# Two score tiles ahead of the first maxima unit in a fused attention and expert kernel

## The chip, the cores and the metric

The kernel runs on one core of one Trainium2 chip. The metric is the device time of one execution in microseconds (us), the median of several. Three executions of the kernel before took 356.44, 356.56 and 356.78 us.

## What is computed

Two layers for a batch of 2. First a cross attention with residual: the 512 tokens of `x` of each batch, normalised, are the queries; keys and values come from the 154 normalised context rows and the same normalised tokens (666 in all), with 16 heads of 64. Then a mixture of 8 experts with residual, where each token goes to its two best experts. The change touches the attention alone, which per batch is

```
q = lat @ Wq;  k, v = split(concat([ctx, lat]) @ Wkv)      # 16 heads of 64
attn = softmax(q @ k.T * 64**-0.5);  x = x + (attn @ v) @ Wout
```

## The kernel before, in words

**Steps.** The attention is worked off in `STEPS` = 16 steps, each a pair of heads of one batch (8 pairs, 2 batches). The scores of a step are kept transposed: keys on the partitions, 512 queries along the free axis. The 666 keys are cut into `KT` = 6 tiles of 111 (`KP`). Each engine runs its own instruction list, written by hand, in order; the lists meet only by semaphores. A step on TensorE has two phases.

**First phase** (L468 to L473). For each key tile `kt`, `dots(s, kt)` (L348) makes the scores of both heads in one of two PSUM buffers, `sc[:, kt % 2]`: six matmuls of 512 columns (L362, two heads of 64 rows each, three products of high and low parts), then two matmuls (L368) that add the negated row maxima of step s. ScalarE then takes the exponent of that tile (`exponent`, L636). Because there are two buffers, `dots(s, kt)` waits at its head until the exponent of tile `kt - 2` is done (L355). After each tile stands one unit of `lead_next(s + 1, u)` (L330, matmuls L326): a rough product of queries and keys of the *next* step, from which VectorE reduces the next step's row maxima (`reduce_max`, L767 and L771). A unit writes `mx` when `u` is even and `xo` when odd. Units 0 to 3 cover 444 keys for 128 queries (two matmuls, one per head); units 4 and 5 cover the other 222 keys for twice 128 queries (four matmuls). From unit 2 on, a unit waits until the reduction of unit `u - 2`, which reads the same buffer, is done (L340: `max_done` at `n * UNITS + u - 1`).

**Second phase.** For steps 0 to 13: `project_q` and `project_k` of step s + 2 (L295 to L297, into the score buffers), then part of a values projection (`project_v`, into `mx`, after the reduction of unit 4, L491). Step 14 has `out_project` (L460, into `mx`) there instead, after the same reduction (L486). Then `turn_max` (L345), which transposes the maxima once VectorE has joined them (`join_max`, L777); `total` (L389); and the six `pv` tiles (L382), the product of exponents and values.

**The other engines in a step.** VectorE: six reductions, `join_max`, low parts of q and k (L751, L758), `spread_max` (L782), four reciprocals (L796). ScalarE: a copy of the previous output (L640), six exponents, copies of q, k and v (L617, L621, L626), a copy of the sums (L646). GpSimd adds up the exponents (`gather`, L1050), normalises (L1057) and splits weights. Step 15 has score tiles but no maxima units between them. After it come the experts.

Of the kernel before, what the change touches and what calls it, by code (L numbers as in the profile page):

```python
# [29 lines left out]
KT = 6  # L30
# [21 lines left out]
def pair_of(s):  # L52
    return 2 * (s // 4) + s % 2
# [6 lines left out]
def v_half(s):  # L60

    n = s // 2 + 1
    return (n, s % 2) if n < STEPS // 2 else None


def v_count(n, half):
    return n * 2 + half + 1


def xattn_moe(nc, x, ctx_in, g_m, b_m, g_l, b_l, wq, wkv, wout, wg, w1, b1, w2, b2, out):  # L70
    with ExitStack() as stack:
# [221 lines left out]
        def _(pe):  # L293
# [5 lines left out]
            def project_q(n, bank=sc[:, 0, 0, :]):  # L299
                b, w = batch_of(n), pair_of(n) % 2  # L300
                three(bank, wqk_hi[:, w, 0, :], wqk_lo[:, w, 0, :], kv_hi[:, b, 0:N], kv_lo[:, b, 0:N]) \
                    .then_inc(q_ready, 1)

            def project_k(n, half, bank):
                b, w = batch_of(n), pair_of(n) % 2
                three(bank[:, 0:k_width(half)], wqk_hi[:, w, 1, :], wqk_lo[:, w, 1, :], kv_hi[:, b, k_cols(half)],
                      kv_lo[:, b, k_cols(half)]).then_inc(k_ready, 1)

            def project_v(n, half, banks=mx):
                b, w = n % B, n // B % 2  # L310
                to = banks.rearrange("p h n -> p (h n)")
                for i in range(VH):
                    kt = half * VH + i
                    at = slice(kt * KP, (kt + 1) * KP)
                    mm = three(to[0:KP, i * 2 * P:(i + 1) * 2 * P], kv_hi[:, b, at], kv_lo[:, b, at],
                               wv_hi[:, w, :], wv_lo[:, w, :])
                mm.then_inc(v_ready, 1)

            def lead(n, u, banks):
                pe.wait_ge(k_hi_done, 2 * n + (1 if u < QT else 2))  # L320
                tiles = [u] if u < QT else [2 * (u - QT), 2 * (u - QT) + 1]
                for i, t in enumerate(tiles):
                    for h in range(2):
                        r = slice(h * HD, (h + 1) * HD)
                        to = banks[:, h, 0:KW] if u < QT else banks[:, h, i * KR:(i + 1) * KR]
                        mm = pe.matmul(to, q_pair[r, n % QKB, 0, t * P:(t + 1) * P],  # L326
                                       k_pair[r, n % QKB, 0, k_cols(u >= QT)], start=True, stop=True)
                mm.then_inc(mx_ready, 1)

            def lead_next(n, u):  # L330
                if u == 0:
                    pe.wait_ge(q_hi_done, n + 1)
                    if n >= 2 and v_half(n - 2):
                        pe.wait_ge(v_copied, v_count(*v_half(n - 2)))
                elif u == 1 and n >= 2:
                    pe.wait_ge(o_copied, n - 1)
                    if n >= 3:
                        pe.wait_ge(sum_copied, n - 2)
                elif u >= 2:
                    pe.wait_ge(max_done, n * UNITS + u - 1)  # L340
                lead(n, u, xo if u % 2 else mx)

            def turn_max(n, bank=sc[:, 1, 1, :]):
                pe.wait_ge(neg_ready, n + 1)
                pe.transpose(bank[:, 0:P], neg_max[:, :, :].rearrange("p h c -> p (h c)"), ident[:, :]) \  # L345
                  .then_inc(neg_turned, 1)

            def dots(s, kt):  # L348
                if kt == 0:
                    later = min(s + 2, STEPS) if s >= 1 else 1  # L350
                    pe.wait_ge(q_lo_done, later)
                    pe.wait_ge(k_lo_done, 2 * later)
                e = s * KT + kt
                if e >= 2:
                    pe.wait_ge(exp_done, e - 1)  # L355
                if kt == 1 and s >= 1:
                    pe.wait_ge(row_done, s + 1)
                at = slice(kt * KP, (kt + 1) * KP)
                for k_part, q_part in ((0, 0), (0, 1), (1, 0)):
                    for h in range(2):  # L360
                        r = slice(h * HD, (h + 1) * HD)
                        pe.matmul(sc[0:KP, kt % 2, h, :], k_pair[r, s % QKB, k_part, at],  # L362
                                  q_pair[r, s % QKB, q_part, :], start=(k_part + q_part == 0), stop=False)
                if kt == 0:
                    pe.wait_ge(row_done, s + 1)
                for h in range(2):
                    r = slice(h * HD, (h + 1) * HD)
                    mm = pe.matmul(sc[0:KP, kt % 2, h, :], ones_r[r, :], max_row[r, s % 2, :],  # L368
                                   start=False, stop=True)
                mm.then_inc(shifted, 1)  # L370
# [15 lines left out]
            def total(s, bank=pj):  # L386
                pe.wait_ge(added, (KT - 1) * (s + 1))
                for h in range(2):
                    mm = pe.matmul(bank[h * HD:(h + 1) * HD, :], ones[0:KP, :], psum_acc[0:KP, s % 2, h, :],  # L389
                                   start=True, stop=True)  # L390
                mm.then_inc(sum_ready, 1)
# [62 lines left out]
            def out_project(b, bank, pairs):  # L454
                pe.wait_ge(o_norm, STEPS - 6)
                for t in range(QT):
                    for r in pairs:
                        if t == 0 and r >= PAIRS - 2:
                            pe.wait_ge(o_norm, (STEPS if b else STEPS - 2) - (PAIRS - 1 - r))
                        mm = pe.matmul(bank[:, t * P:(t + 1) * P], o_t[:, b, r, t * P:(t + 1) * P],  # L460
                                       wout_sb[:, r, :], start=(t == 0 and r == 0),
                                       stop=(t == QT - 1 and r == PAIRS - 1))
                if r == PAIRS - 1:
                    mm.then_inc(out_proj, 1)

            for s in range(STEPS - 1):
                made = s + 2 < STEPS
                for kt in range(KT):  # L468
                    dots(s, kt)
                    if s == 0 and kt == 0:  # L470
                        pe.wait_ge(q_lo_done, 2)
                        pe.wait_ge(k_lo_done, 4)
                    lead_next(s + 1, kt)  # L473
                if made:
                    pe.wait_ge(exp_done, s * KT + KT - 1)
                    if s % 4 in (2, 3):
                        pe.wait_ge(wqk_split, pair_of(s + 2))
                    if s == 0:
                        pe.wait_ge(kv_lo_ready, 2 * B)
                    project_q(s + 2)  # L480
                    project_k(s + 2, 0, sc[:, 0, 1, :])
                    pe.wait_ge(exp_done, s * KT + KT)
                    project_k(s + 2, 1, sc[:, 1, 0, :])
                else:
                    pe.wait_ge(tail_loaded, 16 * 4)
                    pe.wait_ge(max_done, (s + 2) * UNITS - 1)  # L486
                    out_project(0, x1_ps[0], range(PAIRS - 2))
                if v_half(s):
                    if s % 4 == 2:
                        pe.wait_ge(wv_split, s // 4 + 1)  # L490
                    pe.wait_ge(max_done, (s + 2) * UNITS - 1)  # L491
                    if s == 0:
                        project_v(0, 1)
                    else:
                        project_v(*v_half(s))
                pe.wait_ge(exp_done, s * KT + KT)
                turn_max(s + 1)
                if s >= 1:
                    total(s - 1)
                for kt in range(KT):  # L500
                    if s == 0 and kt == VH:
                        pe.wait_ge(v_copied, v_count(0, 1))
                        project_v(1, 0)
                    pv(s, kt)
# [66 lines left out]
            s = STEPS - 1  # L571
# [539 lines left out]
```

## Time and profile before

| what | us |
|---|---|
| median of three executions | 356.56 |
| the profiled execution, device time | 356.89 |
| its span, first to last instruction | 355.1 |
| TensorE matmul busy in the span | 342.6 (96%) |
| VectorE, GpSimd, ScalarE busy | 240.2, 240.7, 181.2 |
| steps 2 to 14, from pv to pv | 16.24 each, step 14 18.9 |

The profile lists for each instruction group when it ran, for how long, and in brackets how long its engine was idle before it and what ended that. PE is TensorE's matmuls, PEld its weight loads, DVE VectorE, ACT ScalarE, POOL GpSimd. Neighbouring matmuls overlap: a matmul of 512 columns is shown as some 0.39 us long while the next of its kind starts 0.23 us after it. So the profile can call TensorE busy throughout and still hold gaps between starts.

### The profile page before, as it was taken

The numbers are of one execution on the slowest core, as the hardware profiler recorded it, in microseconds if no ns is written. First come the engines' busy times: TensorE is split into PE (matmuls) and PEld (weight loads), VectorE is DVE, ScalarE is ACT, GpSimd is POOL, SyncE is SP. The second block draws the span as 40 slices with busy tenths as digits, with TensorE's granted clock in tenths as the row PEclk, the third lists the DMA queues.
The fourth block names the chain that finished last, engine by engine and source line by source line (L and its number), as shares of the span: only waits on it lengthen the run. The fifth ranks groups of instructions, "written<-read, shape, count | busy, mean of one in ns | idle before, by whom it ended". The sixth has DMA issues, their size and how long they took to land.

```text
span 355.1 us, 6060 instructions
## 1 busy us (share of the span) xinstructions
PE 342.6 (96%) x2343; PEld 231.0 (65%) x2343; DVE 240.2 (68%) x418; ACT 181.2 (51%) x240; POOL 240.7 (68%) x160
## 2 busy tenths in 40 slices
PE   2879999999999999999999999999999999999996
PEld 2758574656657474756556474747584559999986
DVE  4789286878677686868686776968744488257433
ACT  2247383755648383836556383838433553135341
POOL 3577586979797989999798989779695661010000
PEclk9999999999999999999999999999999999999999
DMA  3044000000001010010100000000000000000000
GB/s 122 0 145 124 2 14 2 2 2 0 2 0 31 0 31 15 2 30 2 30 3 16 0 2 2 0 2 0 2 0 2 1 0 3 2 0 2 30 2 30
DMA packets 6713, 5.81 MB, mean 16 GB/s; under 512 B 743, under 2 KB 5789, under 8 KB 6685
## 3 DMA queue, kind: packets, MB, share of 16 engines
q1 hardware_dynamic: 6389, 5.29, 5.0%
q8 instruction: 19, 0.31, 0.3%
q10 hardware_dynamic: 296, 0.13, 0.1%
q14 instruction: 9, 0.07, 0.1%
HBM read 4.89 MB, written 0.52 MB: 15 GB/s over the span
## 4 chain that ended last, share of the span: by engine, by line
PE 94%; DVE 3%; DMA 1%; ACT 1%; ACTq 1%; issue 0%; DVEq 0%
PE xo L382 23%; PE sc L362 20%; PE mx L564 8%; PE sc L368 6%; PE sc L295 5%; PE xo L389 5%; PE sc L297 4%; PE sc L296 4%; PE mx L326 3%; PE xo L326 3%; PE mx L460 2%; PE xo L460 2%; PE mx L295 2%; PE mx L297 2%; PE mx L296 2%; DVE part_max L767 1%
## 5 line engine op out<-in xcount | busy, mean ns | idle before, releaser
L1050 POOL TENSOR_TENSOR psum_acc<-psum_acc,probs 111x1024 f32<-111x1024 f32 x63 | 150.0, 2380 | 7.2 <-DVE psum_acc L790 2.5
L636 ACT ACTIVATE probs<-sc 111x1024 f32<-111x1024 f32 x96 | 98.3, 1027 | 21.3 <-PE sc L368 13.9
L362 PE MATMUL sc<-q_pair,k_pair 64*111 64x512 f32 x576 | 85.7, 401 | 1.0 <-ACT v_sb L626 0.8
L382 PE MATMUL xo<-probs,v_sb 111*64 111x512 f32 x384 | 85.6, 593 | 0.0
L362 PEld LDWEIGHTS sc<-q_pair,k_pair 64*111 64x111 f32 x576 | 44.6, 170 | 28.4 <-issue 12.2
L767 DVE TENSOR_REDUCE part_max<-mx 128x2 f32<-128x888 f32 x32 | 34.7, 1084 | 41.0 <-PE mx L326 39.6
L382 PEld LDWEIGHTS xo<-probs,v_sb 111*64 111x64 f32 x384 | 27.3, 137 | 53.6 <-issue 53.2
L796 DVE RECIPROCAL recips<-recips 128x128 f32<-128x128 f32 x64 | 54.3, 910 | 9.4 <-ACT recips L646 9.4
L1050 POOL TENSOR_TENSOR psum_acc<-probs 111x1024 f32<-111x1024 f32 x16 | 38.4, 2398 | 30.7 <-ACT probs L636 30.7
L640 ACT COPY o_t<-xo 128x512 f32<-128x512 f32 x16 | 9.4, 588 | 66.6 <-PE xo L382 66.6
L368 PE MATMUL sc<-max_row,ones_r 64*111 64x512 f32 x192 | 38.1, 390 | 0.0
L703 ACT ACTIVATE probs<-sc,cols 128x512 f32<-128x512 f32 x32 | 21.5, 687 | 28.3 <-PE sc L297 28.0
L767 DVE TENSOR_REDUCE part_max<-xo 128x2 f32<-128x888 f32 x30 | 32.5, 1084 | 1.4
L941 DVE SCALAR_TENSOR_TENSOR x_tok<-mx,score,x_tok 128x128 f32<-128x128 f32 x62 | 17.5, 344 | 22.1 <-PE mx L564 21.9
L564 PEld LDWEIGHTS mx<-w_sb,probs 128*128 128x128 f32 x248 | 29.9, 192 | 2.0 <-issue 0.8
L564 PE MATMUL mx<-w_sb,probs 128*128 128x128 f32 x248 | 30.2, 275 | 0.0
L1057 POOL TENSOR_TENSOR o_t<-o_t,recips 128x512 f32<-128x512 f32 x16 | 20.5, 1278 | 11.2 <-DVE recips L796 11.2
L368 PEld LDWEIGHTS sc<-max_row,ones_r 64*111 64x111 f32 x192 | 16.9, 170 | 5.5
L326 PE MATMUL mx<-k_pair,q_pair 64*128 64x444 f32 (+1 forms) x128 | 18.3, 320 | 1.3 <-DVE part_max L767 0.5
L771 DVE TENSOR_REDUCE part_max<-mx 128x4 f32<-128x888 f32 x16 | 17.3, 1082 | 1.4
L626 ACT COPY v_sb<-mx 111x768 f32<-111x768 f32 x15 | 12.0, 799 | 12.0 <-PE mx L297 12.0
L389 PE MATMUL xo<-psum_acc,ones 111*64 111x512 f32 x64 | 17.3, 618 | 0.0
(169 smaller groups left out, 478.9 us busy)
## 6 DMA issues: line engine op xcount, KB each, us to landing
w_raw<-in_L_ffn_W SPq DMA_DIRECT2D x8, 128.0 KB, 2.0
x_tok<-in_x SPq DMA_DIRECT2D x2, 256.0 KB, 3.4
wv_raw<-in_L_xattn_Wkv SPq DMA_DIRECT2D x4, 128.0 KB, 2.8
wout_sb<-in_L_xattn_Wout SPq DMA_DIRECT2D x1, 512.0 KB
wqk_raw<-in_L_xattn_Wq SPq DMA_DIRECT2D x7, 64.0 KB, 2.0
wqk_raw<-in_L_xattn_Wkv SPq DMA_DIRECT2D x7, 64.0 KB, 2.0
out<-x_tok SPq DMA_DIRECT2D x1, 256.0 KB, 2.0
out<-x_tok SPq DMA_DIRECT2D x2, 128.0 KB, 1.7
```

The lines of the kernel that those rows point to most:

```text
L295: pe.matmul(out_ap, st_hi, mv_hi, start=True, stop=False)
L326: mm = pe.matmul(to, q_pair[r, n % QKB, 0, t * P:(t + 1) * P], k_pair[r, n % QKB, 0, k_cols(u >= QT)], start=True, stop=True)
L362: pe.matmul(sc[0:KP, kt % 2, h, :], k_pair[r, s % QKB, k_part, at], q_pair[r, s % QKB, q_part, :], start=(k_part + q_part == 0), stop=False)
L368: mm = pe.matmul(sc[0:KP, kt % 2, h, :], ones_r[r, :], max_row[r, s % 2, :], start=False, stop=True)
L382: mm = pe.matmul(o_ps[h * HD:(h + 1) * HD, :], v_sb[0:KP, s // 2 % 2, kt, at:at + HD], probs[0:KP, e % RING, h, :], start=(kt == 0), stop= ...
L389: mm = pe.matmul(bank[h * HD:(h + 1) * HD, :], ones[0:KP, :], psum_acc[0:KP, s % 2, h, :], start=True, stop=True)
L564: mm = pe.matmul(y_ps(g, t)[:, t * P:(t + 1) * P], relu_ring[:, (g * HC + c) % FR, t * P:(t + 1) * P], w2_sb[:, e * HC + c, :], start=(c = ...
L636: act.activation(probs[0:KP, e % RING, :, :], sc[0:KP, kt % 2, :, :], ACT.Exp).then_inc(exp_done, 1)
L703: act.activation(relu_ring[:, n % FR, :], hid_ps[:, n % 4, :], ACT.Relu, bias=cols[:, n % (E * HC):n % (E * HC) + 1]).then_inc(relu_done, 1)
L767: dve.tensor_reduce(part_max[:, 0, :, u], banks[:, :, 0:KW], AX.X, ALU.max, negate=True) \
L796: dve.reciprocal(at, at).then_inc(recip_done, 1)
L1050: pool.tensor_tensor(psum_acc[0:KP, s % 2, :, :], first, probs[0:KP, e % RING, :, :], ALU.add) \
```

## The change

In steps 1 to 14 the first phase starts with two score tiles, and each maxima unit stands one place later; the last two units, 4 and 5, follow tile 5 one after the other. Step 0 keeps its order. No instruction is added or removed, and no other engine's list is changed.

```diff
             for s in range(STEPS - 1):
                 made = s + 2 < STEPS
-                for kt in range(KT):
+                ahead = 2 if s else 1
+                for kt in range(ahead - 1):
+                    dots(s, kt)
+                for kt in range(ahead - 1, KT):
                     dots(s, kt)
                     if s == 0 and kt == 0:
                         pe.wait_ge(q_lo_done, 2)
                         pe.wait_ge(k_lo_done, 4)
-                    lead_next(s + 1, kt)
+                    lead_next(s + 1, kt - ahead + 1)
+                if ahead == 2:
+                    lead_next(s + 1, KT - 1)
                 if made:
```

## Rows read from the trace of the kernel before

**Rows 1.** Page: busy time of each engine; chain of work that ended last, by engine
```profile
PE 342.6 (96%) x2343; PEld 231.0 (65%) x2343; DVE 240.2 (68%) x418; ACT 181.2 (51%) x240; POOL 240.7 (68%) x160
...
PE 94%; DVE 3%; DMA 1%; ACT 1%; ACTq 1%; issue 0%; DVEq 0%
```

**Rows 2.** Windows of one step each: length, then busy us of each engine, clock
```profile
74.31:90.56 16.25, 16.25 (x114) 9.81 (x113) 12.27 (x15) 9.51 (x12) 14.21 (x9) 1.00 0.00 1
...
106.80:123.03 16.23, 16.23 (x114) 9.88 (x113) 12.27 (x15) 9.52 (x12) 14.18 (x10) 1.00 0.06 17
```

**Rows 3.** Timeline of one middle step, first phase, TensorE: start us, length us, engine, line
```profile
107.53 0.40 PE L368 MATMUL sc<-max_row,ones_r 64*111 64x512 f32 x2
...
108.89 0.39 PE L326 MATMUL xo<-k_pair,q_pair 64*128 64x444 f32 x2
109.05 0.51 PEld L362 LDWEIGHTS sc<-q_pair,k_pair 64*111 64x111 f32 x6 [0.18 <-ACT probs L636]
109.09 0.91 PE L362 MATMUL sc<-q_pair,k_pair 64*111 64x512 f32 x6
...
112.58 0.85 PE L362 MATMUL sc<-q_pair,k_pair 64*111 64x512 f32 x6
...
113.50 0.38 PE L326 MATMUL xo<-k_pair,q_pair 64*128 64x222 f32 x4
...
113.81 0.50 PE L295 MATMUL sc<-kv_hi,wqk_hi 128*128 128x512 f32 x1
```

**Rows 4.** Chain of waits over the same phase: start of each piece, its length
```profile
107.93 0.20 PE mx L326 x2
108.13 0.70 PE sc L362 x6
108.84 0.23 PE sc L368 x2
109.07 0.20 PE xo L326 x2
109.27 0.73 PE sc L362 x6
...
112.53 0.22 PE mx L326 x4
```

**Rows 5.** Timeline, same step, ScalarE and VectorE in and behind the first phase
```profile
107.97 1.03 ACT L636 ACTIVATE probs<-sc 111x1024 f32<-111x1024 f32 x1 [0.53 <-PE sc L368]
...
112.79 1.08 DVE L771 TENSOR_REDUCE part_max<-mx 128x4 f32<-128x888 f32 x1
...
115.04 0.17 DVE L777 TENSOR_REDUCE neg_max<-part_max 128x8 f32<-128x16 f32 x1
...
116.61 0.27 PE L345 MATMUL sc<-ident,neg_max 128*128 128x128 f32 x1
```

**Rows 6.** Timeline of step 15, two score tiles with no maxima unit between
```profile
272.70 0.39 PE L368 MATMUL sc<-max_row,ones_r 64*111 64x512 f32 x2
...
273.14 1.03 ACT L636 ACTIVATE probs<-sc 111x1024 f32<-111x1024 f32 x1 [0.52 <-PE sc L368]
...
273.63 0.38 PE L368 MATMUL sc<-max_row,ones_r 64*111 64x512 f32 x2
274.21 0.50 PEld L362 LDWEIGHTS sc<-q_pair,k_pair 64*111 64x111 f32 x6 [0.64 <-ACT probs L636]
274.21 0.94 PE L362 MATMUL sc<-q_pair,k_pair 64*111 64x512 f32 x6 [0.20 <-ACT probs L636]
...
275.00 0.40 PE L368 MATMUL sc<-max_row,ones_r 64*111 64x512 f32 x2
```

**Rows 7.** Timeline at the start: a maxima unit held by the reduction before it
```profile
18.66 1.07 DVE L767 TENSOR_REDUCE part_max<-mx 128x2 f32<-128x888 f32 x1
...
19.79 0.48 PE L326 MATMUL mx<-k_pair,q_pair 64*128 64x222 f32 x4 [0.52 <-DVE part_max L767]
20.20 0.44 PE L407 MATMUL sc<-ident,normed 128*128 128x128 f32 x2
```

**Rows 8.** Timeline of step 14, end of its first phase
```profile
258.94 1.08 DVE L771 TENSOR_REDUCE part_max<-mx 128x4 f32<-128x888 f32 x1
...
260.12 0.46 PE L460 MATMUL mx<-wout_sb,o_t 128*128 128x128 f32 x2
```

## The prediction

> **What bounds the kernel now.** I read the page's busy times and its chain first, then windows of single steps, then the timeline of one first phase. TensorE is busy for 342.6 us and carries 94% of the chain that ended last [rows 1]. In the step windows the reader is to see that the matmul row fills all 16.24 us, while the fullest other engine, GpSimd, fills 14.2, VectorE 12.3 and ScalarE 9.5, and that the granted clock is 1.00, the 2.4 GHz level [rows 2]. So a step is as long as TensorE's stream, and a reordering can only win what TensorE loses between starts. The timeline shows where it loses a little: in front of a score tile the weight load was held for the exponent of the tile two before (0.18 us on the load's row), and the matmul behind it began only 0.04 us after the load (109.05 and 109.09) [rows 3]. In the chain the tile so held took 0.73 us for its six matmuls where an unheld one took 0.70 [rows 4]. Four tiles per step can be held in this way, so that there is at most about 0.13 us per step to win.
>
> **What the change moves.** Nothing is added: the same matmuls and weight loads, no DMA, no queue other than TensorE's. Tile 1 goes ahead of unit 0; units 0 to 4 each come one place later; units 4 and 5 meet at the end. The wait that tile 1 carries for the spread maxima is met by then, as tile 0's last matmuls wait for the same semaphore. That edit costs nothing. I follow the times of the middle step of rows 3.
>
> *Hold one, tile 2 behind exponent 0.* Tile 0's last matmuls end at 107.53 + 0.40 = 107.93 [rows 3]; exponent 0 runs from 107.97 for 1.03, to 109.00 [rows 5]. Neither moves. Tile 1 now follows at once. Step 15 already has this order, and there tile 1's last matmuls start 273.63 - 272.70 = 0.93 after tile 0's [rows 6]. So here they start at 108.46. Unit 0 starts 0.23 later (the chain's step of a score pair [rows 4]), at 108.69, and tile 2 could start 0.20 after that (the chain's step of a unit), at 108.89. But it must wait for exponent 0. Before, the load that was so released started at 109.05 [rows 3], 0.05 after the exponent's end; in step 15 it was 274.21 against 273.14 + 1.03 = 274.17 [rows 6]. So tile 2 starts at 109.05, the very time of before. A tile that starts from a hold needs, by step 15, 275.00 + 0.40 - 274.21 = 1.19 to its end [rows 6], so tile 2 ends at 110.24; before, its pieces ended at 109.27 + 0.73 + 0.23 = 110.23 [rows 4]. The time saved by having one unit less ahead of tile 2 is thus lost whole, and the unit has still to be paid: every later tile keeps its time, and the phase ends with one unit more. Cost: the 0.20 that a unit takes in the chain, per step. Bounds: nothing at all if tile 2 could start without the hold, 0.30 if the restart from a longer stop is worse than in step 15. I take 0.20.
>
> *Tiles 3 to 5.* After tile 2 the stream is again tile, unit, tile, with units 1, 2, 3 in the places where 2, 3, 4 stood. Exponent 1 may start up to 0.2 earlier, which removes a hold of some hundredths at tile 3; exponent 2 and tile 4 hang on tile 2's end and do not move. I count the gain at nothing; what hides it is the chain tile 2, exponent 2, tile 4, and at most 0.05 per step would come out.
>
> *Hold two, unit 5 behind the reduction of unit 3.* Unit 3 now sits behind tile 4, where unit 4's four short matmuls were, which in the chain started at 112.53 [rows 4]. Unit 3 ends there at 112.53 + 0.20 = 112.73. Its reduction starts 0.04 later (unit 4's did: 112.53 + 0.22 = 112.75 against 112.79) and takes 1.08 [rows 5]: to 113.85. Unit 4 starts at 113.50 in the place of unit 5 [rows 3], and its own reduction to wait for, of unit 2, ended over a unit's pitch before, near 112.7: free. Unit 5 could start 0.21 later, at 113.71, but needs the reduction of unit 3. The nearest row for such a release is the start of the kernel, where a reduction ended at 18.66 + 1.07 = 19.73 and the held unit started at 19.79 [rows 7]. So unit 5 starts at about 113.90: a hold of 0.19. And its restart is slow: there the next instruction started 20.20 - 19.79 = 0.41 after the held unit [rows 7], where a flowing one gives 113.81 - 113.50 = 0.31 [rows 3]. So `project_q` starts at 113.90 + 0.41 = 114.31 and not at 113.81: 0.50 later in all, 0.20 from hold one and 0.30 from hold two. For hold two the bounds are 0 (if the reduction were already done) and 0.40; I take 0.30. Queued behind unit 5 on TensorE is everything of the second phase, and ScalarE's and VectorE's copies of q and k wait for that.
>
> *A rule on restarts.* In the row of step 15 the matmul of a held tile and its weight load carry the same start, 274.21, and the load engine had been idle for 0.64 [rows 6]: the weights were not loaded during the hold. The Trainium skill, page "TensorE: Matmul & The Clock Gate", section "Step-by-step: what each phase is for", says that TensorE's queue pulls weight loads ahead of matmuls in flight. Were that so behind a hold as well, both restarts would lose the 0.10 of slow start, and the sum would fall to 13 x 0.30 + 1.1 = 5.0. The row speaks against it, as the wait sits ahead of the load.
>
> *Second phase.* The reductions of units 4 and 5 come late: unit 4 ends at about 113.88, its reduction runs to 114.99, unit 5's to 116.1, and the join of 0.17 ends near 116.3 instead of 115.21 [rows 5]. The transpose of the maxima stood at 116.61 [rows 5] and stands at 117.11 now, so that 0.8 are left. The values projection before it needs the reduction of unit 4 (114.99) and starts after 115.9. Both waits stay hidden. The reciprocals and the spreading end over 3 us before VectorE is wanted again. GpSimd, with 14.2 of 16.2, gets more room. Nothing in the second phase can give the 0.50 back, as TensorE's row has no wait there.
>
> *Step 14* has the output projection behind unit 5, which waits for the reduction of unit 4. Before, that ran from 258.94 to 260.02 and the matmuls started at 260.12 [rows 8], already held. Now unit 4 takes unit 5's place, whose start in the chain's terms is 1.13 later; its reduction ends at 261.15 and the projection starts at 261.25. Cost 1.13, which contains both holds. Bounds 0.20 and 1.3.
>
> **Sum.** Steps 1 to 13: 13 x 0.50 = 6.5. Step 14: 1.1. Together 7.6 us. On the profiled execution, 356.89 (its span 355.1 and 1.8 around it), that is 364.5; it was 0.33 above the median, so against the median 364.2.
>
> **The rivals.**
>
> *A: both holds, as above,* 364.2; its own range is 362.5 to 365.5 (0.1 per step either way on 14 steps). Chance 0.76.
>
> *B: only hold one.* If the reductions ran a little ahead of what I reconstruct, unit 5 would find its buffer free. For: VectorE is busy for only 12.3 of 16.2 [rows 2]. Against: the reduction of unit 3 cannot start before unit 3 is computed, and 1.08 behind that is later than 113.71. Time: 13 x 0.20 + 1.1 = 3.7, so 360.3. Chance 0.08.
>
> *C: restarts cost nothing,* as the rule above would have it: 5.0, so 361.6. Chance 0.05.
>
> *D: faster.* In ends rather than starts hold one hardly exists: exponent 0 ends 0.04 + 1.03 after tile 0, and tile 1 with unit 0 takes 0.93 + 0.20, so that tile 2 would just find it done. If the hold were then no more than the ones of before, each later tile would run unheld and the 0.13 per step of small holds would come out: 14 x 0.13 = 1.8, so 354.8. It decides from the point at which exponent 0 is visible before 108.89. Against it speaks step 15, where the held start follows the exponent's end by 0.04 although the matmuls before were still draining. Chance 0.05.
>
> *E: worse.* The join of the maxima, 1.1 later on VectorE, becomes what TensorE waits for at the transpose. It decides once the join ends after 117.1, that is if the 0.8 of slack is lost, for instance because VectorE starts on q's low part first; its list excludes that order, but a further slip of each reduction would do. Price another 0.5 per step, so 371. Chance 0.06.
>
> **Chances and range.** A difference of 0.2% (0.7 us) is about what a measurement of this kernel can tell from none. Faster by more: 0.05, all of D. Within it: 0.02, between D and B. Slower: 0.93. The range of 360.2 to 366.2 holds A, B and C and leaves out D and E.
>
> **What would show it.** Right: a step of 16.74 in place of 16.24; in each middle first phase one idle of TensorE of about 0.2 ahead of tile 2, ended by the exponent (L636), and one of about 0.2 ahead of unit 5 (L326 on `xo`), ended by the reduction (L767); the first phase's length 7.57 in place of 7.07; step 14's projection (L460) starting 1.1 later relative to its step. Wrong: tile 2 starting before 109.0 relative to this step (D), unit 5 with no idle ahead of it (B), a new wait at L345 (E), the unheld pitch right behind a hold (C). A step that isn't longer than 16.24 would overturn the whole argument.

## The result and the profile after

| | before | changed |
|---|---|---|
| median of 6 executions, us | 356.67 | 364.49 |
| lowest, highest | 356.44, 356.82 | 364.37, 366.59 |
| step pitch, steps 1 to 13 | 16.24 | 16.75 |
| step 14, sums of step 13 to sums of step 14 | 19.02 | 20.19 |

The ratio is 1.0229, with a 95% interval of 1.0217 to 1.024: slower by 7.8 us, where 7.6 had been forecast (364.2). The pitch is read from the chain of waits, where each step's `total` is one piece. The first and the last of the thirteen pieces that bound twelve steps are, after the change, with step 14's behind them,

```profile
54.37 1.01 PE xo L389 x4
...
255.33 1.01 PE xo L389 x4
...
275.52 1.01 PE xo L389 x4
```

so (255.33 - 54.37) / 12 = 16.75; before, the same pieces start at 51.94 and 246.81. The twelve steps are 2 to 13; step 1, from its first tile to its sums, takes 10.60 against 10.10 before, so it loses the same. 13 x (16.75 - 16.24) + (20.19 - 19.02) = 7.8, the whole of the measured difference. That the two agree to a tenth is in part luck: step 1's first tile starts at 41.77 in the profile before and at 41.25 in that of a later run, `not_in_step_14`, whose step 0 is the same, so the start of the kernel alone differs by half a microsecond from one profiled execution to another. Behind step 14 the two kernels take the same time: from step 15's first tile to the end 83.2 us before, 83.1 after.

The page after, busy times and chain, answers to [rows 1]:

```profile
PE 351.5 (96%) x2343; PEld 233.1 (64%) x2343; DVE 237.7 (65%) x418; ACT 179.9 (49%) x240; POOL 240.7 (66%) x160
...
PE 93%; DVE 3%; DMA 1%; ACT 1%; issue 1%; ACTq 1%; DVEq 0%
```

One step's window after, answering to [rows 2]: 16.71 of 16.75 us are called busy. The extra half microsecond shows as almost no idle, because a held matmul's predecessor is drawn as still running.

```profile
77.25:94.00 16.75, 16.71 (x113) 9.87 (x113) 12.08 (x15) 9.41 (x12) 14.13 (x9) 1.00 0.00 1
```

The timeline of the same middle step, 3.92 us later on this trace's clock than in [rows 3] (start, length, engine, line, in brackets the idle before and what ended it):

```profile
111.88 1.95 ACT L641 ACTIVATE probs<-sc 111x1024 f32<-111x1024 f32 x2 [0.52 <-PE sc L368]
112.37 0.39 PE L368 MATMUL sc<-max_row,ones_r 64*111 64x512 f32 x2
112.60 0.36 PE L326 MATMUL mx<-k_pair,q_pair 64*128 64x444 f32 x2
112.96 0.94 PE L362 MATMUL sc<-q_pair,k_pair 64*111 64x512 f32 x6
...
112.96 0.50 PEld L362 LDWEIGHTS sc<-q_pair,k_pair 64*111 64x111 f32 x6 [0.40 <-ACT probs L641]
...
116.69 1.08 DVE L772 TENSOR_REDUCE part_max<-xo 128x2 f32<-128x888 f32 x1
...
117.42 0.38 PE L326 MATMUL mx<-k_pair,q_pair 64*128 64x222 f32 x4
117.83 0.30 PEld L326 LDWEIGHTS xo<-k_pair,q_pair 64*128 64x128 f32 x4 [0.22 <-DVE part_max L772]
117.83 0.48 PE L326 MATMUL xo<-k_pair,q_pair 64*128 64x222 f32 x4
...
118.24 0.50 PE L295 MATMUL sc<-kv_hi,wqk_hi 128*128 128x512 f32 x1
```

Both holds stand where the forecast put them. Unit 0 starts at 112.60 and tile 2 not 0.20 but 0.36 later, at 112.96; less 3.92 that is 109.04, within 0.01 of the time at which its load was released before (109.05). Unit 5 starts 0.41 after unit 4 and not 0.21; the reduction of unit 3 ended at 117.77. The projection follows unit 5 by 0.41: 118.24, less 3.92 114.32, where the forecast had 114.31 and the kernel before 113.81.

The chain tells it by pieces; against [rows 4], where a held tile took 0.73:

```profile
112.76 0.20 PE mx L326 x2
112.97 0.94 PE sc L362 x6
...
117.58 0.21 PE mx L326 x4
117.79 0.04 issue
117.83 0.48 PE xo L326 x4
```

### The profile page after: what moved, and what is told of

It reads as the page before. It is cut to its first block, busy times and chain, and to the rows that moved or that the text cites. A ratio compares the mean times of both kernels' runs of the same rounds, so it can differ in the third digit from the quotient of the medians.

```text
span 364.8 us, 6060 instructions
## 1 busy us (share of the span) xinstructions
PE 351.5 (96%) x2343; PEld 233.1 (64%) x2343; DVE 237.7 (65%) x418; ACT 179.9 (49%) x240; POOL 240.7 (66%) x160
## 4 chain that ended last, share of the span: by engine, by line
PE 93%; DVE 3%; DMA 1%; ACT 1%; issue 1%; ACTq 1%; DVEq 0%
PE xo L382 23%; PE sc L362 20%; PE mx L569 7%; PE sc L368 6%; PE sc L295 5%; PE xo L389 4%; PE sc L297 4%; PE sc L296 4%; PE xo L326 4%; PE mx L326 3%; PE mx L460 2%; PE xo L460 2%; PE mx L295 2%; PE mx L297 2%; PE mx L296 1%; DVE part_max L772 1%
## 5 line engine op out<-in xcount | busy, mean ns | idle before, releaser
L641 ACT ACTIVATE probs<-sc 111x1024 f32<-111x1024 f32 x96 | 96.9, 1027 | 23.6 <-PE sc L368 18.6
L362 PE MATMUL sc<-q_pair,k_pair 64*111 64x512 f32 x576 | 87.3, 408 | 0.9 <-ACT v_sb L631 0.7
L362 PEld LDWEIGHTS sc<-q_pair,k_pair 64*111 64x111 f32 x576 | 45.9, 173 | 33.4 <-issue 12.2
L326 PE MATMUL xo<-k_pair,q_pair 64*128 64x444 f32 (+1 forms) x120 | 18.0, 338 | 0.5
```

What stands on the lines that cost most here:

```text
L641: act.activation(probs[0:KP, e % RING, :, :], sc[0:KP, kt % 2, :, :], ACT.Exp).then_inc(exp_done, 1)
```

## The experiments

My theory: the loss of a step is the sum of two holds, hold one of tile 2 behind exponent 0 (0.20) and hold two of unit 5 behind the reduction of unit 3 (0.30 with its restart), and step 14 pays for the late reduction of unit 4. Rivals were a price of the order itself (two tiles or two units side by side), and holds that overlap. Each time below stands beside the kernel before, which was 356.8 beside them.

**The pair of units moved to after tile 2.** In place of the change's loop, for this and the next experiment with k = 2 and k = 1:

```diff
-                ahead = 2 if s else 1
-                for kt in range(ahead - 1):
-                    dots(s, kt)
-                for kt in range(ahead - 1, KT):
+                unit = 0
+                for kt in range(KT):
                     dots(s, kt)
...
-                    lead_next(s + 1, kt - ahead + 1)
-                if ahead == 2:
-                    lead_next(s + 1, KT - 1)
+                    for _ in range(1 if s == 0 else {0: 0, k: 2}.get(kt, 1)):
+                        lead_next(s + 1, unit)
+                        unit += 1
```

> The order of the change, but units 1 and 2 both follow tile 2, so that only unit 0 and unit 1 stand one place later and the last units stand as before. Theory of two holds: hold one (tile 2 behind exponent 0) stays with 0.20 us per step, hold two (unit 5 behind the reduction of unit 3) is gone, unit 2 just finds its reduction done. 14 x 0.20 = 2.8 over 356.7, so 359.4; step pitch 16.44. Rival, the cost comes from a phase that ends with two units: then this is as fast as before, 356.7. Rival, every displaced unit waits a little for its reduction: a third of the loss, 359.3 as well, but with idles ended by VectorE and none by ScalarE.

Measured 363.67, ratio 1.018 (1.0146 to 1.0214), pitch 16.72. The expectation missed by 4.3 us. The timeline of the pair's neighbourhood shows why:

```profile
112.10 0.36 PE L326 MATMUL xo<-k_pair,q_pair 64*128 64x444 f32 x2
112.27 0.19 PEld L326 LDWEIGHTS mx<-k_pair,q_pair 64*128 64x128 f32 x2 [0.21 <-DVE part_max L770]
112.30 0.45 PE L326 MATMUL mx<-k_pair,q_pair 64*128 64x444 f32 x2
...
112.51 1.08 DVE L770 TENSOR_REDUCE part_max<-xo 128x2 f32<-128x888 f32 x1 [0.29 <-PE xo L326]
112.58 0.85 PE L362 MATMUL sc<-q_pair,k_pair 64*111 64x512 f32 x6
...
113.28 0.40 PE L368 MATMUL sc<-max_row,ones_r 64*111 64x512 f32 x2
...
113.65 0.47 PE L326 MATMUL xo<-k_pair,q_pair 64*128 64x444 f32 x2
```

Unit 1 is made at 112.10, its reduction ends at 113.59, and unit 3, which writes the same buffer and would have come 0.23 after the matmuls of 113.28, at 113.51, starts at 113.65 and restarts slowly: the tile behind it comes 0.31 later (113.96) in place of 0.20. Unit 2, on time at 112.30, had its load held for the reduction of unit 0, and the tile behind it comes 0.28 later. I had followed units 2 and 0 and not unit 3 and unit 1. So the hold by a reduction isn't special to the end of the phase: a unit needs some 1.5 us from its start to that of the one two places on (0.36 for itself, 1.08 for the reduction, and the two handovers), and where two units meet with no tile between, one tile is missing from that room.

**The pair after tile 1.**

> Units 0 and 1 both follow tile 1, and from tile 2 on all is as before; the two score tiles still stand together. Theory: tile 2 has its old distance from tile 0, so no idle ended by the exponent ahead of it, and the unheld pitch; but unit 0 is computed 0.9 later, its reduction ends near 110.17 on the scale of the middle step, and unit 2, two places behind, is held by 0.2 and restarts 0.1 slowly; some 0.1 comes back from exponent holds that vanish. 14 x 0.2 = 2.8, so 359.5, with the idle ended by VectorE (L772). Rival, the exponent is all that matters in a first phase: 356.7 or up to 0.05 less per step, 356.0.

Measured 360.36, ratio 1.0089 (1.0056 to 1.0123), pitch 16.51, with 0.27 lost per step where I had said 0.2. The trace shows unit 2 held, by VectorE:

```profile
125.78 0.37 PE L326 MATMUL mx<-k_pair,q_pair 64*128 64x444 f32 x2
...
126.19 1.08 DVE L770 TENSOR_REDUCE part_max<-mx 128x2 f32<-128x888 f32 x1 [3.38 <-PE mx L326]
...
126.98 0.39 PE L368 MATMUL sc<-max_row,ones_r 64*111 64x512 f32 x2
...
127.32 0.19 PEld L326 LDWEIGHTS mx<-k_pair,q_pair 64*128 64x128 f32 x2 [0.43 <-DVE part_max L770]
127.33 0.47 PE L326 MATMUL mx<-k_pair,q_pair 64*128 64x444 f32 x2
```

Unit 2 comes 0.35 after tile 2's last matmuls in place of 0.23, and the tile behind it 0.30 later in place of 0.20: 0.22 of the 0.27. Tile 2 itself takes 0.80 in the chain, and the 0.1 that I had expected back didn't come. Tile 2 no longer pays hold one, but the reduction holds unit 2: this kernel has hold two's kind alone, and the rival that only the exponent matters falls.

**Hold two taken out of the changed kernel.** `n` is the step whose maxima are reduced, one ahead of the step that TensorE is in, so the short reduction acts from step 1 on.

```diff
-                    dve.tensor_reduce(part_max[:, 0, :, u], banks[:, :, 0:KW], AX.X, ALU.max, negate=True) \
+                    dve.tensor_reduce(part_max[:, 0, :, u], banks[:, :, 0:KW // 2 if u == 3 and n >= 2 else KW], AX.X, ALU.max, negate=True) \
```

> The changed kernel, but the reduction of unit 3 reads only half of its 444 columns in steps 2 and later; it leaves out the maxima over the other half. Theory: that reduction takes about 0.6 us in place of 1.08, unit 5 finds its buffer free, 0.30 per step come out of steps 1 to 13 and step 14 keeps its loss: 364.5 - 13 x 0.30 = 360.6, step pitch 16.45. Rival, the end of the phase is slow because two units of four short matmuls stand together: 364.5 stays.

Measured 360.75, ratio 1.0109 (1.0067 to 1.0151), pitch 16.46. The shortened reduction takes 0.62, and unit 5 now follows unit 4 by 0.21 with no idle, as the timeline has it:

```profile
113.36 0.62 DVE L772 TENSOR_REDUCE part_max<-xo 128x2 f32<-128x444 f32 x1
...
114.10 0.38 PE L326 MATMUL mx<-k_pair,q_pair 64*128 64x222 f32 x4
...
114.31 0.39 PE L326 MATMUL xo<-k_pair,q_pair 64*128 64x222 f32 x4
...
114.63 0.50 PE L295 MATMUL sc<-kv_hi,wqk_hi 128*128 128x512 f32 x1
```

Hold two is thus worth 0.28 per step (16.747 - 16.463), and two units side by side cost nothing in themselves.

**Hold one taken out.**

```diff
-                act.activation(probs[0:KP, e % RING, :, :], sc[0:KP, kt % 2, :, :], ACT.Exp).then_inc(exp_done, 1)
+                w = N // 2 if kt == 0 and 2 <= s < STEPS - 1 else N
+                act.activation(probs[0:KP, e % RING, :, 0:w], sc[0:KP, kt % 2, :, 0:w], ACT.Exp).then_inc(exp_done, 1)
```

> The changed kernel, but in steps 2 to 14 the exponent of tile 0 is taken of half of its queries only; it leaves out the other half. That activation takes about 0.6 us in place of 1.03. Theory: tile 2 no longer waits for it, hold one goes, hold two stays, as unit 3 and its reduction come as much earlier as the rest: 13 steps (step 14 too) x 0.2 = 2.6, of which some hundredths per step may come back as a hold of tile 3 behind exponent 1, so 362.0, step pitch 16.57. Rival, the tile's place next to another tile is what costs: 364.5 stays.

Measured 361.82, ratio 1.0147 (1.0106 to 1.0189), pitch 16.53: 0.21 per step. The timeline of one step (tile 1's last matmuls, unit 0, tile 2 and its last matmuls):

```profile
127.82 0.60 ACT L642 ACTIVATE probs<-sc 111x512 f32<-111x512 f32 x1 [0.51 <-PE sc L368]
...
128.30 0.40 PE L368 MATMUL sc<-max_row,ones_r 64*111 64x512 f32 x2
...
128.53 0.36 PE L326 MATMUL mx<-k_pair,q_pair 64*128 64x444 f32 x2
...
128.73 0.92 PE L362 MATMUL sc<-q_pair,k_pair 64*111 64x512 f32 x6
...
129.49 0.40 PE L368 MATMUL sc<-max_row,ones_r 64*111 64x512 f32 x2
```

Tile 2 now starts 0.20 after unit 0 and not 0.36: nothing holds it. But from its start to its last matmuls it takes 0.76, where an unheld tile takes 0.69 (127.61 to 128.30 for tile 1 here). Those 0.07 are not the hold of tile 3 that I had expected: nothing holds a load, but the pairs of matmuls from tile 2's first to its last start 0.24, 0.25 and 0.27 apart (128.73, 128.97, 129.22, 129.49) in place of 0.23. No run explains that. In another step of the same trace tile 2 takes 0.69, and there the expected hold shows: tile 3's load waits for the exponent of tile 1, and the tile takes 0.74 in the chain.

```profile
113.34 0.50 PEld L362 LDWEIGHTS sc<-q_pair,k_pair 64*111 64x111 f32 x6 [0.20 <-ACT probs L642]
```

The steps of either kind are equally long (16.5 us), and the next kernel has both kinds too at the pitch of the kernel before, so neither is a loss that the order brings.

**Both taken out.**

> The changed kernel with both shortenings, exponent 0 on half of its queries and the reduction of unit 3 on half of its columns. Theory: the holds add up, so both going brings 13 x 0.48 back and leaves step 14's wait for the reduction of unit 4: 358.4, step pitch near 16.26. Rival, the holds overlap, and taking one of them lets another wait take its place: above 360.

Measured 358.00, ratio 1.0032 (1.0017 to 1.0047), pitch 16.25, so that 0.50 of the 0.51 is gone. The two holds add up. What is left is step 14, 19.97 in place of 19.02: 0.95 of the 1.2 us by which this kernel is slower than the kernel before.

**Step 14 left in its old order.**

```diff
-                ahead = 2 if s else 1
+                ahead = 2 if 0 < s < STEPS - 2 else 1
```

> The changed kernel with step 14 left in its old order. Theory: the 1.17 us that step 14 lost come back, as its projection waits for the reduction of unit 4: 364.5 - 1.2 = 363.3. Rival, that wait is made up for by later slack and the tail is as long in any case: 364.5 - 0.5 = 364.0.

Measured 363.34, ratio 1.0171 (1.0137 to 1.0205), 1.15 less than the changed kernel, with step 14 back at 19.04. Nothing behind it makes up for the wait: from step 15's first tile to the end is 83.1 us in the changed kernel too.

**Short reductions with the pair moved.** The kernels of the first two runs have full reductions after all:

> Units 1 and 2 behind tile 2, with the reductions of units 0 to 3 reading half of their 444 columns from step 2 on. Its counterpart with full reductions took 363.7, not the 359.4 expected, and its trace shows units 2 and 3 held by the reductions of units 0 and 1. Theory mended: any two units without a tile between them bring such a hold, and without it only hold one is left: 0.20 x 14 = 2.8, so 359.5, step pitch 16.44. Rival, the place of the pair after tile 2 costs by itself: 363.7 stays.

> Units 0 and 1 behind tile 1, with the same short reductions. Theory: with neither the exponent nor a reduction in the way a step falls back to its old 16.24, less up to 0.1 for exponent holds that vanish: 356.0, between 355.3 and 356.9. Rival, two score tiles without a unit between cost TensorE something in themselves: 358 or more.

They are repeats of the two kernels with the pair after tile 2 and tile 1, and gave 363.55 and 360.19 where these had given 363.67 and 360.36. They say nothing on what was expected of them; the kernels meant follow, with, for every n from step 2 on,

```diff
-                    dve.tensor_reduce(part_max[:, 0, :, u], banks[:, :, 0:KW], AX.X, ALU.max, negate=True) \
+                    dve.tensor_reduce(part_max[:, 0, :, u], banks[:, :, 0:KW // 2 if n >= 2 else KW], AX.X, ALU.max, negate=True) \
```

> Units 1 and 2 behind tile 2, the reductions of units 0 to 3 reading half of their 444 columns from step 2 on (the other half is left out). Theory: two units without a tile between them bring a hold by a reduction; with short reductions only hold one is left: 0.20 x 14 = 2.8, so 359.5, step pitch 16.44. Rival, the place of the pair after tile 2 costs by itself: 363.6 stays.

Measured 359.32, ratio 1.0062 (1.0039 to 1.0084), pitch 16.42. This is hold one alone, 0.18 per step, and in its chain tile 2 takes 0.92 while the pair flows:

```profile
109.76 0.92 PE sc L362 x5
110.68 0.23 PE sc L368
110.91 0.21 PE xo L326 x2
111.11 0.20 PE mx L326 x2
111.32 0.69 PE sc L362 x6
```

> Units 0 and 1 behind tile 1, with the same short reductions. Theory: with neither the exponent nor a reduction in the way a step falls back to its old 16.24, less up to 0.1 for exponent holds that vanish: 356.0, between 355.3 and 356.9. Rival, two score tiles without a unit between cost TensorE something in themselves: 358 or more.

Measured 356.71, ratio 0.9996 (0.9985 to 1.0008), pitch 16.23. With neither hold, two tiles and two units side by side cost nothing. The gain of up to 0.1 per step that I had allowed for didn't come. The loads of tiles 2 and 4 are still held for a moment by the exponent:

```profile
124.95 0.50 PEld L362 LDWEIGHTS sc<-q_pair,k_pair 64*111 64x111 f32 x6 [0.17 <-ACT probs L639]
...
127.24 0.50 PEld L362 LDWEIGHTS sc<-q_pair,k_pair 64*111 64x111 f32 x6 [0.20 <-ACT probs L639]
```

> The kernel before with the same short reductions (units 0 to 3 read half of their columns from step 2 on). Theory: no reduction holds TensorE in the old order, so nothing is won: 356.7, step pitch 16.24. Rival, the reductions already set the pace of the old order in part, and the gain of the short ones in the other kernels is only that: 355 or less.

Measured 356.73, ratio 0.9996 (0.9984 to 1.0008), pitch 16.24. The short reductions win nothing in the old order, so what they won elsewhere is the hold and not a faster VectorE.

| kernel | hold one | hold by a reduction | pitch | us |
|---|---|---|---|---|
| before; before with short reductions | no | no | 16.24; 16.24 | 356.8; 356.73 |
| pair after tile 1, short reductions | no | no | 16.23 | 356.71 |
| changed, both shortened | no | no, but step 14's | 16.25 | 358.00 |
| pair after tile 2, short reductions | yes | no | 16.42 | 359.32 |
| changed, short reduction of unit 3 | yes | no, but step 14's | 16.46 | 360.75 |
| pair after tile 1 | no | unit 2 | 16.51 | 360.36 |
| changed, short exponent 0 | no | unit 5, step 14's | 16.53 | 361.82 |
| pair after tile 2 | yes | units 2 and 3 | 16.72 | 363.67 |
| changed | yes | unit 5, step 14's | 16.75 | 364.49 |

No order tried is faster than the kernel before.

## Why the prediction was right, step by step

*Bound.* TensorE's stream sets the step; right. What it lost went to the total one for one: 7.8 by steps, 7.8 measured, with the luck told above.

*Hold one* was put at 0.20. It measured 0.21 with the exponent shortened and 0.18 with the reductions out of the way. Tile 2 started at 109.04 on the old scale, forecast 109.05. The row that made this safe was step 15's, where the order already existed: rival D, which counted by ends and gave a gain, needed a start before 109.0. One argument against D was misread: in step 15 the matmuls ahead of the held tile were not draining any more, they had ended at 273.63 + 0.38 = 274.01, and the row has 0.20 of idle. It is the changed kernel that shows the case: exponent 0 ends at 112.91 while unit 0 is drawn until 112.96, and tile 2 starts at 112.96, 0.05 after the exponent and 0.36 after unit 0, where it follows a unit by 0.20 if nothing holds it. And A's own range, 0.1 per step either way on 14 steps, should have read 362.8 to 365.6.

*Tiles 3 to 5* at nothing; right. From the end of tile 2 to unit 4 the chain takes 3.44 (114.14 to 117.58), before 3.43 (110.23 to 113.66). The possible gain from vanishing small holds came in no run.

*Hold two* at 0.30, of which 0.19 wait and 0.10 restart. Measured 0.28 by shortening the reduction; the row shows 0.22 of idle on the load. Rival B (no hold two) would have read 360.3, and 360.75 is what the kernel took once that hold was removed, so its price was right to 0.2 (3.9 above the kernel before, where it had 3.7) and its condition was not met.

*Restart.* The load of tile 2 starts at 112.96, the very start of its matmul, and the tile then takes 0.94 in the chain. The wait stands ahead of the load as well, and rival C's 361.6 didn't come. The Trainium skill has weights pulled ahead of matmuls in flight (page "TensorE: Matmul & The Clock Gate", section "Step-by-step: what each phase is for"); in this trace that does not reach past a wait, as load and matmul start together at 112.96.

*Second phase.* I had the join end 0.8 before the transpose needs it. In the timeline after it ends at 119.94 + 0.17 = 120.11, and the transpose stands at 121.06:

```profile
119.94 0.17 DVE L782 TENSOR_REDUCE neg_max<-part_max 128x8 f32<-128x16 f32 x1
...
121.06 0.27 PE L345 MATMUL sc<-ident,neg_max 128*128 128x128 f32 x1
```

So 0.95 was left, and rival E had no ground.

*Step 14* at 1.13; measured 1.17 in the changed kernel's own trace, 1.15 by leaving it out. The forecast said that this contains both holds. Hold one it does: with the short exponent 0 the step takes 19.95 in place of 20.19. Hold two stands behind unit 4 and is hidden by the wait for its reduction: with hold two gone the step still takes 20.15. Its rows after, answering to [rows 8]:

```profile
268.63 1.08 DVE L776 TENSOR_REDUCE part_max<-mx 128x4 f32<-128x888 f32 x1
...
269.81 0.91 PE L460 MATMUL mx<-wout_sb,o_t 128*128 128x128 f32 x6 [0.71 <-issue]
```

The reduction of unit 4 ends at 269.71 and the projection starts 0.10 later, as before. The idle is put down to "issue", but with both holds taken out the step still takes 19.97, and with its old order 19.04. Where units 4 and 5 keep their old places (pair after tile 1, short reductions) it takes 19.00.

What stays open: why tile 2's matmuls are 0.07 slower in some steps than in others, and whether the small holds could be had. The holds seem to come from a round of tile, exponent and the tile two on: in the kernel with the pair after tile 1 and short reductions the two held loads start 2.29 apart (124.95 and 127.24), where unheld tiles and units would take 2.24 (twice 0.20 + 0.69 + 0.23). That is argued from these rows and no run takes it apart.

## What to carry to other kernels

When two engines hand work back and forth through two buffers, count for each buffer the time from the start of one use to the earliest start of the next, and set it beside the work that lies between, the round of that buffer; moving an item by one place takes its length out of the work that covers one such round, and the item itself has still to be done. Look in the trace for a place where the new order already runs, here the last step: its rows gave hold one, start and restart, to 0.01 us. Check every round that the moved item is in and not only the ones at the ends: the one expectation that missed by much followed one buffer and forgot the other.

## What the runs showed of the hardware beyond that

Two exponents back to back took 1.95 us, not 2 x 1.03 (first row of the timeline above), and back to back reductions of 1.08 started 1.00 apart: in the timeline after the change,

```profile
117.83 1.08 DVE L776 TENSOR_REDUCE part_max<-mx 128x4 f32<-128x888 f32 x1
...
118.83 1.07 DVE L776 TENSOR_REDUCE part_max<-xo 128x4 f32<-128x888 f32 x1
```

I had laid the reductions end to end. That is most of the 0.15 of extra slack at the join, which ended at 116.19 on the old scale and not near 116.3; the transpose stood 0.03 later than forecast.

The profiled execution of the changed kernel took 366.59, 2.1 over the median of its six executions. Its windows show the granted clock down at the 1.2 GHz level in step 0, which the change doesn't touch; before, it was 1.00 there:

```profile
20.00:24.00 4.00, 3.64 (x26) 3.26 (x24) 2.84 (x4) 1.49 (x3) 2.93 (x5) 0.77 0.43 120
24.00:26.00 2.00, 1.32 (x7) 0.80 (x8) 1.29 (x3) 0.80 (x1) 1.39 (x3) 0.50 1.11 320
26.00:28.00 2.00, 2.00 (x14) 1.37 (x12) 1.08 (x3) 0.64 (x1) 0.00 (x0) 0.50 1.06 293
```

In the first 20 us TensorE had been busy for 11.97, but for 12.06 in the kernel before, whose clock stayed at 1.00; so these figures don't say what brought the clock down. One more profile, of the kernel with the short exponent (363.77 against a median of 361.82), shows the same dip (0.77 from 20 to 24 us, 0.58 from 24 to 30). All step times above lie behind it.
